# Loading the features before the first adjacency tile, and transposing that tile last in the opening of a graph network kernel

## The reference, cut to what matters

```
def _L0_gnn_ref(x, support, weight):
    bw = sign(weight)                 # 256 x 256
    ba = maximum(sign(x), 0.0)
    xw = ba @ bw.T
    return relu(support @ xw)
x = _layernorm(x + _L0_gnn_ref(x, adj, L0_gnn_weight))
```

## Time and profile before

| what | value |
|---|---|
| median of 3 runs | 515.81 us (514.64 to 516.01) |
| the profiled execution | 513.07 us, of which its span is 511.3 us |
| PE busy | 482.5 us, 94% of the span |
| DVE, ACT, POOL busy | 345.6, 244.9, 172.8 us |
| mean granted clock of TensorE | 0.986 |

### The profile page before, as it was taken

One profiled execution on the slowest core, in us unless ns is written; L12 is line 12 of the kernel. 1 busy time (PEld: TensorE's weight loads), 2 busy tenths in 40 slices (PEclk: granted clock), 3 DMA queues, 4 the chain that ended last, 5 costly groups with the idle time before them and its releaser, 6 DMA issues.

```text
span 511.3 us, 5688 instructions
## 1 busy us (share of the span) xinstructions
PE 482.5 (94%) x1901; PEld 304.3 (60%) x1901; DVE 345.6 (68%) x747; ACT 244.9 (48%) x450; POOL 172.8 (34%) x175
## 2 busy tenths in 40 slices
PE   5999999999999989999999999999999999999890
PEld 4899755455555778876545446555556545554580
DVE  4789879999862879475237647935623794576776
ACT  5767369974885543333335424424324664342300
POOL 1422423542332068632004414502310462424511
PEclk9999999999999999999999999999999999999895
DMA  9856300000543000000000000000000000000101
GB/s 308 242 176 187 108 2 0 0 0 9 210 159 91 1 1 0 1 1 1 0 0 1 0 1 0 2 0 0 1 0 0 1 1 2 0 0 0 42 21 47
DMA packets 8148, 20.68 MB, mean 40 GB/s; under 512 B 976, under 2 KB 4708, under 8 KB 8120
## 3 DMA queue, kind: packets, MB, share of 16 engines
q1 hardware_dynamic: 6840, 18.75, 11.1%
q0 software_dynamic: 464, 0.79, 0.8%
q10 hardware_dynamic: 816, 0.79, 0.5%
HBM read 18.94 MB, written 1.39 MB: 40 GB/s over the span
## 4 chain that ended last, share of the span: by engine, by line
PE 82%; DVE 8%; ACT 3%; issue 3%; POOL 2%; DMA 1%; POOLq 0%; ACTq 0%; DVEq 0%
PE psum L1457 18%; PE psum L1504 15%; PE psum L1239 10%; PE psum L1275 9%; PE psum L1335 5%; PE psum L1222 4%; PE psum L1437 4%; PE psum L1575 3%; PE psum L1294 2%; PE psum L1410 2%; PE psum L1539 2%; PE psum L1156 2%; PE psum L1321 1%; PE psum L1389 1%; PE psum L1486 1%
## 5 line engine op out<-in xcount | busy, mean ns | idle before, releaser
L1457 PE MATMUL psum<-QT,xT 128*128 128x512 f32 (+3 forms) x264 | 107.7, 543 | 0.3 <-DVE xT L1027 0.3
L1504 PE MATMUL psum<-ST,Wh 128*128 128x512 f32 (+3 forms) x220 | 94.9, 563 | 1.6 <-DVE vbuf L1009 1.1
L410 POOL TENSOR_TENSOR es<-es,ST 128x512 f32<-128x512 f32 (+3 forms) x60 | 72.3, 1204 | 59.2 <-ACT ST L613 57.5
L600 ACT ACTIVATE ST<-psum 128x512 f32<-128x512 f32 (+3 forms) x66 | 36.0, 546 | 86.2 <-DVE rm L960 80.9
L1457 PEld LDWEIGHTS psum<-QT,xT 128*128 128x128 f32 (+1 forms) x264 | 48.2, 186 | 47.2 <-issue 40.7
L960 DVE TENSOR_TENSOR rm<-psum,rm 128x512 f32<-128x512 f32 (+3 forms) x60 | 37.3, 622 | 46.8 <-PE psum L1457 46.8
L1504 PEld LDWEIGHTS psum<-ST,Wh 128*128 128x128 f32 (+1 forms) x220 | 40.8, 190 | 40.4 <-issue 33.2
L360 POOL TENSOR_TENSOR rstd<-veps,nhalf 128x1 f32<-128x1 f32 (+1 forms) x44 | 29.3, 667 | 95.0 <-DVE veps L767 94.9
L1275 PE MATMUL psum<-eb,x_all 128*128 128x512 f32 (+3 forms) x132 | 52.8, 545 | 0.0
L982 DVE TENSOR_TENSOR ST<-ST,psum 128x512 f32<-128x512 f32 (+3 forms) x66 | 39.9, 614 | 17.6 <-PE psum L1486 17.6
L613 ACT ACTIVATE ST<-ST 128x512 f32<-128x512 f32 (+3 forms) x66 | 37.8, 579 | 27.6 <-DVE ST L982 25.0
(11 more groups left out here) (165 smaller groups left out, 757.0 us busy)
## 6 DMA issues: line engine op xcount, KB each, us to landing
adj_rows<-in_adj_dram SPq DMA_DIRECT2D x10, 677.0 KB, 5.0
rows<-in_adj_dram SPq DMA_DIRECT2D x10, 677.0 KB, 4.1
out_dram<-xs SPq DMA_DIRECT2D x10, 128.0 KB, 1.7
x_all<-in_x_dram SPq DMA_DIRECT2D x2, 512.0 KB, 6.7
W<-in_L_gnn_W_stack_dram SPq DMA_DIRECT2D x2, 512.0 KB, 5.6
adj_rows<-in_adj_dram SPq DMA_DIRECT2D x1, 338.5 KB
rows<-in_adj_dram SPq DMA_DIRECT2D x1, 338.5 KB
w0n<-in_L_gnn_weight_dram ACTq DMA_DIRECT2D x1, 256.0 KB, 5.1
```

Of the source, the lines that this page charges most:

```text
L410: nc.gpsimd.tensor_tensor(es[0:r, g % 2, 0:w], es[0:r, g % 2, 0:w], buf(g)[0:r, j, 0:w], ALU.add)\
L600: nc.scalar.activation(buf(g)[0:r, j, 0:w], psum[0:r, SB[n % 3], 0:w], ACT.Copy).then_inc(st_ready.sem, 1)
L1457: last = nc.tensor.matmul(psum[0:r, SB[n % 3], 0:w], xT[l][:, k, j * P:j * P + r], QT[:, k, c0:c1], start=(k == 0), stop=(k == KD - 1))
L1504: last = nc.tensor.matmul(bank(AB[g] + m, 0, w), Wh[g // NC][0:r, j, m * P:(m + 1) * P], buf(g)[0:r, j, 0:w], start=(j == 0), stop=(j == T ...
```

## The change

On SP the three feature groups and the tail are issued first, and tile 0 of `adj` behind them, in one run with the other tiles. On PE the weight's transposes stand behind `turn_pos(0)`, and `adj_turn(0)` behind `mul_pos(2)`, just before `adj_turn(1)`. On DVE `positive(0)` is ahead of the weight's signs, and `lower_bits(0)` behind the three copies of `xw`. On ACT `adj_evac(0)` stands behind the loop over `posT`, ahead of the issue of `Wsa` and of `xw_evac(3)` and `xw_evac(5)`. Nothing is added or removed.

```
@@ SP
-            load_rows(0)
             for g in range(BANKS_T):
                 ...  # features, three groups, then the tail in two
-            for i in range(1, FULL):
+            for i in range(FULL):
                 load_rows(i)
@@ ACT
-            adj_evac(0)
             act.wait_ge(w0T_ps.sem, 1)
             nc.scalar.activation(w0T[:, :, :], bankb(7)[:, 0:KD * D].rearrange("p (k n) -> p k n", k=KD),
...
                 if g == 1:
                     xw_evac(1)
+            adj_evac(0)
             act.dma_start(Wsa[:, :, :], w_sa.rearrange("(k p) n -> p k n", p=P)).then_inc(wsa_in.sem, 16)
             xw_evac(3)
             xw_evac(5)
@@ DVE
-            (wait for w0_in, w0neg, w0s)
             positive(0)
+            (wait for w0_in, w0neg, w0s)
             positive(1)
             positive(2)
-            lower_bits(0)
             for t0 in range(0, T, 4):
                 ...  # copies of xw
+            lower_bits(0)
             lower_bits(1)
@@ PE
-            pe.wait_ge(pads_zero.sem, 1)
-            adj_turn(0)
-            (wait for w0_signed, four transposes of w0s)
             turn_pos(0)
+            (wait for w0_signed, four transposes of w0s)
             turn_pos(1)
             mul_pos(0)
             turn_pos(2)
             mul_pos(1)
             mul_pos(2)
+            pe.wait_ge(pads_zero.sem, 1)
+            adj_turn(0)
             adj_turn(1)
```

More of the change, by code:

```diff
@@ L729, in _ @@
             own.link(nc.vector.memset(Ub[:, :, :, :], 0.0))
[L731 to L734, removed]
             def lower_bits(i, groups=range(BANKS_T)):
@@ L750, in _ @@
             positive(0)
+            dve.wait_ge(w0_in.sem, 16)
+            own.link(nc.vector.tensor_scalar(w0neg[:, :, :], w0n[:, :, :], 0.0, None, ALU.is_lt))
+            nc.vector.scalar_tensor_tensor(out=w0s[:, :, :], in0=w0n[:, :, :], scalar=0.0, in1=w0neg[:, :, :],
+                                           op0=ALU.is_gt, op1=ALU.subtract).then_inc(w0_signed.sem, 1)
             positive(1)
             positive(2)
-            lower_bits(0)
             for t0 in range(0, T, 4):
@@ L1158, in adj_turn @@
                     last.then_inc(adjT_turned.sem, 1)
[L1160 to L1167, removed]
             def turn_pos(g):
@@ L1192, in _ @@
             turn_pos(0)
+            pe.wait_ge(w0_signed.sem, 1)
+            w0T_v = bankb(7)[:, 0:KD * D].rearrange("p (k n) -> p k n", k=KD)
+            for o in range(KD):
+                for k in range(KD):
+                    last = nc.tensor.transpose(w0T_v[:, k, o * P:(o + 1) * P], w0s[:, o, k * P:(k + 1) * P], identb[:, :])
+            last.then_inc(w0T_ps.sem, 1)
             turn_pos(1)
```

## The result

The changed kernel takes 520.13 us in the median of 12 runs (517.63 to 522.26), the kernel before 515.22 us beside it (12 runs, 513.12 to 517.70). The ratio is 1.0085, with a 95% interval of 1.0057 to 1.0113: slower by 4.4 us between the means (2.9 to 5.8; the medians are 4.9 apart), where 4.0 were forecast and a median of 519.8. The profiled execution has a span of 516.0 us against 511.3, which is 4.7 more, at the same mean granted clock of 0.986.

What follows compares the result with a forecast made beforehand. PE, busy 94% of the span, was taken as the bound, with any delay of `adj_turn(1)` passed on nearly one to one. 3.04 us plus 1.0 for the clock, 4.0 on 515.81, gave 519.8 us; range 517.4 to 521.6.

Steps and rivals of the forecast that it cites:

- landmark: Start of the steady sequence, `agg_a(3)` on PE: forecast at 32.3 to 33.3 us instead of 29.21.
- The earlier projection: Opening: with features loaded first, `mul_pos(0)` starts at 9.65 us instead of 10.59, 0.95 us gained.
- The six copies in front of `xw_evac(3)`: ACT's opening: `adj_evac(0)`'s copies precede `xw_evac(3)`, so `adj_turn(1)` starts at 16.73 us, 3.04 us later than before.
- The clock: PE's clock falls after its 2.6 us wait and slows `adj_turn(1)`: 1.0 us, bounds 0 to 1.2.
- a fall in the wait: PE's clock drops after idling ahead of `adj_turn(1)`; nine of its 11 transposes run slowly, 1.0 us.
- Rival 2: Clock rises late in the opening, slowing `mul_pos(0)` by 0.9 us, and also falls at the wait: 520.7 us; chance 0.20.
- late rise: PE's clock still low in the opening, so `mul_pos(0)`'s 8 matmuls run slowly: 0.9 us more, or 2.0 with following work.
- The sum: Opening's delay of `adj_turn(1)`, passed on nearly one to one: 3.04 us plus 1.0 for PE's clock, 4.0 us.
- rival 1: PE's clock holds at the wait ahead of `adj_turn(1)`: only 3.0 us slower, 518.8 us; chance 0.33.
- What was costed at nothing: Later `Wsa`, tile 3 and POOL's `a_b` transfers land before use: no cost, with 4 us of margin or more.
- POOL as the link: At 15 us: POOL's transfers wait for `adj_turn(1)`, so its 1.6 us of slack absorbs nothing of the delay.
- Rival 3: ACT's order does not hold `adj_turn(1)`, which follows `adj_turn(0)` without a gap: about +0.5 us, 516.3 us; chance 0.05.

Runs made afterwards that it cites:

- e1: Changed kernel with `xw_evac(3)` and `xw_evac(5)` put ahead of `adj_evac(0)` on ACT; ratio to the kernel before 1.0033 (1.0006 to 1.0060).
- e5: Changed kernel with tile 0 loaded first again, so the engines' orders alone; ratio to the kernel before 1.0088 (1.0055 to 1.0121).
- e7: Changed kernel without POOL's wait for `adj_turn(1)`; steady sequence starts 1.48 us earlier in the profile, no timed ratio given.
- e2: Changed kernel with 19 added transposes of the identity at PE's start; ratio to the kernel before 1.0053 (1.0021 to 1.0085).
- e8: Changed kernel with 19 added transposes at PE's start and 22 between `adj_turn(0)` and `adj_turn(1)`; ratio to the kernel before 1.0075 (1.0044 to 1.0106).
- e11: Kernel before with 18 added transposes in PE's wait near 478 us, opening untouched; ratio to the kernel before 1.0009 (0.9985 to 1.0032).
- e6: Kernel before without POOL's wait for `adj_turn(1)`; median 514.97 us against 515.93, ratio 0.9983 (0.9960 to 1.0007).
- e9: Changed kernel with `xw_evac(3)` and `xw_evac(5)` ahead of `adj_evac(0)` on ACT and 19 added transposes at PE's start; ratio 1.0035 (1.0003 to 1.0068).
- e10: Kernel before without POOL's wait for `adj_turn(1)` and with 18 added transposes in PE's wait near 478 us; ratio 0.9988 (0.9961 to 1.0014).

## Why the prediction was right, point by point

| step | forecast | changed kernel |
|---|---|---|
| `positive(0)` starts | 5.4 | 5.40 |
| `mul_pos(0)` starts | 9.65 | 9.42 |
| `adj_turn(0)` starts | 12.74 | 14.25 |
| `adj_turn(1)` starts | 16.73 | 18.36 |
| PE's wait ahead of it | 2.6 | 2.74 |
| cost of the clock | 1.0, in `adj_turn(1)` | 1.7, in `mul_pos` |
| POOL's first `Wg` | 18.4 to 19.4 | 20.06 |
| landmark | 32.3 to 33.3 | 33.90 |

- **The earlier projection** was right: 10.59 - 9.42 = 1.17 us gained, 0.95 forecast. The `w0T` copy started at 7.85 instead of 8.0.
- **The six copies in front of `xw_evac(3)`** were right: from `adj_turn(0)` to `adj_turn(1)` 18.36 - 14.25 = 4.11 us, against 3.99. The 0.12 us more stand in the chain as the issue of `Wsa`. e1 shows that this order is the cause, by taking it away: the wait of 2.74 us is gone.
- **The clock** is the term that was wrong. The forecast put 1.0 us on a fall in the wait; in the profiled execution `adj_turn(1)` took 1.39 us and no fall came, nor did it after the same wait in e5 and e7; only in e2 did it. Instead the clock rose late. Rival 2 had the late rise, but together with the fall, so no case of the forecast is the one that came: `mul_pos` from first to last took 14.25 - 9.42 = 4.83 us against 13.69 - 10.59 = 3.10, so 1.73 us, where the rival priced 0.9 with a bound of 2.0. e2 and e8 show both mechanisms, 1.9 and 1.0 us. Which of them an execution meets differs, and e11 meets the late rise without the change. That a term of 1.0 us for one reason stood where another reason gave some 1.7 is luck, as far as the total goes.
- **The sum**: -1.17 + 1.73 + 4.11 = 4.67, and the landmark moved by 4.69. Without the clock's term it would be 2.94, against 3.04 forecast; like for like the landmark moved by 2.69 and 2.81. The part of the forecast that the change's own mechanism carries, a delay of 3.04 us through ACT's queue, is thus borne out by the traces a little short. By it alone the forecast would have been 518.8 us (rival 1), against 520.13 measured.
- **What was costed at nothing** was hidden: `Wsa` landed in 4.6 us and was not waited for at its first use, and no tile of `adj` was waited for behind the opening.
- **POOL as the link**: too narrow, as e6 and e7 show, without effect on the sum.
- **The Trainium skill's rule** (TensorE: Matmul & The Clock Gate, "Part 4: PE-mode transpose"), that transposes do not count for the clock, is against the trace once more: in e8 PE did nothing but transposes up to 9.27 us, and the eight matmuls that began there took 1.05 us. Transposes alone can bring the clock up, then; in e9, with the same ones, it was down again by 9.23 us.
- **Rival 3**, not slower, fell with e1: the wait was on ACT's order.

## What to carry to other kernels

When a block of work is moved behind another, look at which in-order queue it then heads: six copies of 2.7 us in all held the copy of `w0T` for at most 0.8 us while they headed ACT's queue (it started at 8.96 us, its transposes were done at 8.17), and cost 2.33 us of the kernel once PE waited for the next item of that queue. Work that needs only an early transfer is worth most in the time in which nothing else can run; doing it later puts its whole length in front of something. And lay two kernels' traces side by side at the first point from which they run alike, rather than by their ends; and before a difference between two traces is put down to an edit, look whether untouched executions differ by as much at the same place, as they do here with the late rise (2.0 us).

## What the runs showed of the hardware

- The clock's first rise came late in some executions and in time in others of the same opening: `mul_pos(0)` took 1.05 us in the kernel before and in e6, 1.89 in e10 and e11.
- PE's clock can rise, fall and rise within the first 13 us. In e9 it fell with no idle stretch over 0.78 us, in a stretch in which PE was busy for 1.71 us of 3. In e2 it fell after an idle stretch of 2.74 us, and in the changed kernel, e5 and e7 after the same wait it did not.
- The same program differs by up to 5.6 us between executions (512.97 to 518.62 for the kernel before). Its executions beside these experiments took 513.0 to 515.2 us where the mean granted clock was 0.986, and 517.7 to 518.0 where it was 0.976 to 0.977; the longest, 518.62, had 0.980, so the mean clock is not the whole of it. A part of it is around 170 to 180 us: the stretch 165 to 185 us had a mean clock of 1.00 in the kernel before and 0.74 in e6, with PE busy for more than 19 of the 20 us in both. That is why spans of single executions were not compared above.

```profile
165.00:185.00 20.00, 19.14 (x95) 14.11 (x93) 13.42 (x46) 10.78 (x22) 2.06 (x3) 1.00 0.00 0
```

```profile
165.00:185.00 20.00, 19.77 (x78) 14.57 (x77) 11.15 (x38) 9.09 (x17) 0.55 (x1) 0.74 0.00 0
```

The first row is the kernel before, the second e6; PE's busy time is the second number. What decides there whether the clock falls stays open.
